# Last spline of a graph network: records loaded once the points have used them, GpSimd waiting for the spreads itself, and late picks standing in front of the wait for a spread

## What is computed

```
new_pseudo = jnp.clip(pseudo + t[col] - t[row], 0.0, 1.0)
basis2, idx2 = spline_basis(new_pseudo)        # 3 coordinates, 5 hats each: 125 weights, 8 of them not zero
z = jnp.einsum('ni,kio->nko', x, W)            # W: [125, 32, 32]
msg = jnp.einsum('es,eso->eo', basis, z[col * 125 + idx])
out = segment_sum(msg, row) / max(degree, 1) + b
```

## Time and profile before

| what | us |
|---|---|
| median of 3 runs (range) | 6453.58 (6439.67 to 6467.0) |
| the profiled execution, its own time | 6460.42 |
| its span, first to last instruction | 6458.6 |
| first gather of this stage starts | 5155.21 |
| first gather after it that waited for a load (block 7) | 5371.20 |
| last gather of this stage starts, takes | 6347.66, 0.94 |
| first `pos` of block 0, of block 1 | 5215.94, 5238.55 |
| first `pos` of block 36, the last | 6379.35 |

### The profile page before, as it was taken

How to read it: one execution, slowest core, us unless ns; L and a number is a source line. 1 busy time by engine, 2 the same in 40 slices (tenths; PEclk the granted TensorE clock), 3 DMA queues, 4 the chain that set the end, 5 groups by cost and what they waited for, 6 DMA issues and landing times. The chain is left out here.

```text
span 6458.6 us, 112027 instructions
## 1 busy us (share of the span) xinstructions
PE 4758.0 (74%) x38171; PEld 3579.6 (55%) x38171; DVE 4337.5 (67%) x11010; ACT 1867.2 (29%) x3181; POOL 4196.4 (65%) x4245
## 2 busy tenths in 40 slices
PE   5444444493668988888885755999999678888885
PEld 4444444363656766666664343555555366666664
DVE  7665565366888877777773222777777477788875
ACT  0212111254884444444442000000000033333332
POOL 1777777406946777777772533777777377777773
PEclk9999999987999999989887877999999889999998
DMA  4222222014442222222223946111111211111110
GB/s 69 87 74 79 81 74 71 18 34 118 169 164 49 58 59 57 58 55 57 58 55 101 325 142 189 38 38 37 37 37 37 37 19 22 22 22 22 22 22 16
DMA packets 387137, 441.07 MB, mean 68 GB/s; under 512 B 244355, under 2 KB 310736, under 8 KB 386397
## 3 DMA queue, kind: packets, MB, share of 16 engines
q1 hardware_dynamic: 202041, 290.11, 14.3%
q0 software_dynamic: 128224, 124.94, 11.5%
q10 hardware_dynamic: 56528, 21.19, 1.6%
HBM read 354.14 MB, written 82.34 MB: 68 GB/s over the span
## 5 line engine op out<-in xcount | busy, mean ns | idle before, releaser
L886 POOL DMA_INDIRECT ar_far<-att_table,ar_rec x1184 | 1210.4, 1022 | 422.8 <-issue 352.6
L1726 POOL DMA_INDIRECT p_far<-table,p_rec x888 | 866.2, 975 | 417.3 <-issue 262.2
L2564 PE MATMUL g_l_ps_sum<-g_l_row,g_l_of 128*128 128x392 f32 x3224 | 1064.5, 493 | 19.4 <-DVE g_l_of L2515 19.4
L2486 POOL DMA_INDIRECT g_l_got<-table,g_l_index x806 | 812.6, 1008 | 245.5 <-issue 227.8
L550 POOL DMA_INDIRECT rec_r<-so_r_rec,so_r_place x806 | 788.1, 978 | 245.5 <-issue 245.2
L2564 PEld LDWEIGHTS g_l_ps_sum<-g_l_row,g_l_of 128*128 128x128 f32 x3224 | 613.9, 190 | 470.5 <-DVE g_l_of L2515 20.5
L1500 PE MATMUL at_bank<-p_spread,p_basis 64*125 64x256 f32 x4736 | 624.1, 410 | 99.1 <-ACT p_outer L1562 99.1
L505 PE MATMUL so_r_look<-so_r_table,so_r_lo_t 128*128 128x26 f32 x1612 | 424.9, 434 | 313.2 <-DVE so_r_table L447 313.2
L2498 DVE TENSOR_SCALAR g_l_row<-g_l_iota,edge_row 128x784 f32<-128x784 f32 x806 | 500.4, 694 | 230.9 <-PE g_l_ps_sum L2564 230.8
L1500 PEld LDWEIGHTS at_bank<-p_spread,p_basis 64*125 64x125 f32 x4736 | 525.4, 196 | 179.3 <-ACT p_outer L1562 122.8
L1562 ACT COPY p_outer<-at_bank 125x512 f32<-125x512 f32 x1184 | 592.2, 715 | 101.2 <-PE at_bank L1500 100.6
(11 more groups left out here) (493 smaller groups left out, 6946.6 us busy)
## 6 DMA issues: line engine op xcount, KB each, us to landing
adjacent<-ad_by_chunk SPq DMA_DIRECT2D x74, 800.0 KB, 3.3
so_r_row<-pad_src SPq DMA_DIRECT2D x62, 832.0 KB, 6.1
g_l_counts<-adjacent SPq DMA_DIRECT2D x60, 800.0 KB, 7.1
g_l1d_counts<-adjacent SPq DMA_DIRECT2D x59, 800.0 KB, 6.8
so_r_low<-pad_lo_src SPq DMA_DIRECT2D x62, 416.0 KB, 4.6
ar_far<-att_table,ar_rec POOLq DMA_INDIRECT x1184
p_far<-table,p_rec POOLq DMA_INDIRECT x888
rec_r<-so_r_rec,so_r_place POOLq DMA_INDIRECT x806
```

The lines of the kernel that those rows point to most:

```text
L886: pool.indirect_dma_start(out=self.far[q][:, t, :], out_offset=None, in_=self.g.att_table[:, :], in_offset=bass.IndirectOffsetOnAxis(ap=se ...
L1726: pool.indirect_dma_start(out=sl.far[b][:, t, :], out_offset=None, in_=table[:, :], in_offset=bass.IndirectOffsetOnAxis(ap=sl.rec[b][:, t, ...
L2486: pool.indirect_dma_start(out=got[b][:, j, :], out_offset=None, in_=table[:, :], in_offset=bass.IndirectOffsetOnAxis(ap=index[b][:, j:j + ...
L2564: last = nc.tensor.matmul(ps_sum[k][:], of4[b][:, j, :, :].rearrange("p k f -> p (k f)"), row1[b][:, j, k * COLS:(k + 1) * COLS], start=Fa ...
```

## The change

Three edits in this stage, none of them in arithmetic:

1. In `outer_products`, the late picks (tiles 8 and 20) are issued before TensorE waits for the spread of these tiles, where they stood behind that wait.
2. SP loads block `n`'s records as soon as `positions` says that the points of block `n - 3` have read them, where it waited for that block's last spread.
3. GpSimd, from block 3 on, waits itself for the spreads of block `n - 3` (the readers of `far[b]`) after it has waited for the records. Its first three blocks are therefore written out ahead of its loop, and the loop starts at lap 1.

```diff
             if t % self.HT == 0:
                 pe.wait_ge(self.bases, m * 2 + (t // self.HT + 1))
+            if late is not None and t in (8, 20):
+
+                late[0].pick(pe, m + 1, 2 + (t == 20))
             if t % self.XT == 0:
                 pe.wait_ge(self.spreads, m * self.XS + (t // self.XT + 2))
...
             if turn_of is not None and t == self.HT - self.BT:
                 self.turn(pe, turn_of)
-            if late is not None and t in (8, 20):
-
-                late[0].pick(pe, m + 1, 2 + (t == 20))
...
                 with sp.Fori(1, turns) as i:
                     for b in ring:
-                        sp.wait_ge(sl.spreads, i * (R * sl.XS) + ((b - R + 1) * sl.XS + 1))
+                        sp.wait_ge(sl.positions, i * R + (b - R + 2))
                         sl.load(sp, i * R + b, b)
                 for n in range(turns * R, o.blocks):
-                    sp.wait_ge(sl.spreads, (n - R + 1) * sl.XS + 1)
+                    sp.wait_ge(sl.positions, n - R + 2)
                     sl.load(sp, n, n % R)
...
-                def gather(i, b):
+                def gather(i, b, first=False):
                     pool.wait_ge(sl.loaded[b], i * sl.loads + sl.loads)
+                    if not first:
+                        pool.wait_ge(sl.spreads, i * (R * sl.XS) + ((b - R + 1) * sl.XS + 1))
                     pool.sem_inc(taken, 1)
...
-                with pool.Fori(0, turns) as i:
+                for b in ring:
+                    gather(0, b, first=True)
+                with pool.Fori(1, turns) as i:
                     for b in ring:
                         gather(i, b)
```

## The result

| | before | changed |
|---|---|---|
| median (range) | 6456.01 us (6439.67 to 6467.0), 4 runs | 6397.74 us (6390.22 to 6399.57), 4 runs |
| ratio of the medians, 95% interval | | 0.9904 (0.9886 to 0.9923) |
| the profiled execution, its span | 6460.42, 6458.6 | 6390.22, 6388.2 |
| first gather of the stage | 5155.21 | 5144.57 |
| `pos` of block 1, of block 36 | 5238.55, 6379.35 | 5226.52, 6309.27 |

The kernel became faster by about 58 us where 74 were forecast, and the time lies inside the range. The spans differ by 70.4 us, but 10.6 of them lie ahead of the stage, which no edit touches: in the profiled executions of this study its first gather starts anywhere from 5132.02 to 5168.05. From here on I compare the 35 blocks between the `pos` of block 1 and that of block 36 ("the 35 blocks"): they lost 58.05 us, and the tail behind them kept its 79 us.

What follows compares the result with a forecast made beforehand. DVE and PE, waiting on each other through the late picks, were taken as the bound, GpSimd hidden. Waits 59 plus clock 15 gave 74 us off the profiled 6460.4, so 6386, median 6379; range 6360 to 6410.

Steps and rivals of the forecast that it cites:

- waits for spreads before picks: PE's waits for DVE's spreads ahead of late picks, 81.8 us over the stage, would go, less what stays or comes new.
- the new wait for spread 3: On PE ahead of tiles 12 to 15: 0.4 us a block in 22 blocks, as DVE makes one-hots before that spread.
- Edit 1: Late picks on PE start sooner: block 15 falls from 33.04 to 29.4 us, the stage gains 59 + 15 = 74.
- The clock: PE's picks return from half to full clock after shorter idleness: 15 us of gain, bounds 22 and −15.
- The 22 us in picks 2: Time lost to half clock in the picks 2 of 15 blocks that followed a long wait on PE.
- The factor of 0.7: Share taken of the clock's 22 us, giving 15, since block 16 shows PE meeting half clock elsewhere too.
- Rival 1: PE falls to half clock at the loop's start or another pick as often: gain 42 to 62 us, chance 0.22.
- Edits 2 and 3: Loads and GpSimd's wait: up to 64.9 us of POOL's idleness go, but by themselves they are worth nothing.
- Rival 2: GpSimd's wait costs more than SP's and bounds: 6396 us at 0.8 a block; chance 0.08 part, 0.03 slower.
- The cap: GpSimd's gather work ends no sooner than 6291.9, so block 36's points start 6298 to 6301: gain at most 78 to 85 us.
- Rival 3: Something other than the pick, such as ScalarE, holds tiles 20 to 23: gain 20 to 40 us, chance 0.09.
- Rival 4: Order of picks does nothing because kept products come as late as the spreads: time 6454, chance 0.03.

Runs made afterwards that it cites:

- edit 1 alone: Kernel before with only the late picks issued ahead of the wait for their spread, loads and GpSimd's wait as before: 6392.03 us, ratio 0.9893.
- the laps of six: Changed kernel with TensorE's loop written out for six blocks a lap instead of three: 6395.53 us, ratio 0.9896 against the kernel before.
- the shifts ahead: Changed kernel with the near shifts and the turn also issued ahead of the wait for spread 3 at tile 12: 6384.76 us, ratio 0.9879.
- the one-hots later: Kernel with near shifts and turn ahead of tile 12's wait, VectorE making one-hots behind spread 3 instead of ahead: 6382.25 us, ratio 0.9871.
- pick 3 late again: Changed kernel with tile 20's pick back behind the wait for its spread, tile 8's still ahead: 6416.23 us, ratio 0.9924.
- filling the gap before pick 2: Kernel before, products of tile 7 issued eight times over in all but a lap's first block: 6455.80 us, ratio 0.9981.

## Why the prediction was right, and where 16 us went

The sum can be checked term by term against groups by line, of the kernel before from 5238 to 6380 us (two that the earlier trace rows doesn't hold):

```profile
L1500 PE MATMUL p_ps_outer<-p_spread,p_basis 64*125 64x128 f32 x4510 | 316.1, 284 | 35.5 <-issue 25.3 <-DVE p_spread L1434 7.3
...
L1528 PE MATMUL p_ps_rest<-p_fold,p_run 128*128 128x32 f32 x140 | 22.1, 281 | 0.0
```

and of the changed kernel from 5226 to 6310 us:

```profile
L1680 PE MATMUL p_pick_ps_pick<-p_pick_parts,p_pick_turned_hot 128*128 128x245 bf16 x3360 | 398.7, 276 | 71.6 <-DVE p_pick_kept L1653 71.6
L1500 PE MATMUL p_ps_outer<-p_spread,p_basis 64*125 64x128 f32 x4510 | 313.4, 283 | 31.0 <-issue 22.8 <-DVE p_spread L1434 6.0
L1528 PE MATMUL p_ps_rest<-p_fold,p_run 128*128 128x32 f32 x140 | 23.4, 292 | 0.0
L1464 PE MATMUL p_ps_rest<-p_shift,mask_t 8*128 8x96 f32 x70 | 15.9, 306 | 30.3 <-DVE p_spread L1434 30.2
```

| term | forecast | measured |
|---|---|---|
| waits for spreads before picks, gone | 81.8 | 81.8 |
| more waiting for kept products (71.6 − 57.2) | −22 × 0.65 = −14.3 | −14.4 |
| the new wait for spread 3 | −22 × 0.4 = −8.8 | −30.2 |
| idleness ahead of products (35.5 − 31.0) | 0 | 4.5 |
| clock: picks 13.4, products 2.7, turn −1.3 | 15 | 14.8 |
| sum | 74 | 56.5 |

Of the 58.05 us that the blocks lost, 1.5 aren't attributed by this.

**Edit 1: the mechanism was right.** Pick 2 waits at most 0.71 us for a kept product, spread 4 doesn't stall, and the gain comes from PE starting late picks sooner. **The step that failed in size** is "Here a new wait stands: spread 3 ends at 5718.44, ... so PE waits 0.4 us". I let the near shifts and the turn run beside this wait, though in the code they stand behind it, and they take 0.94 us. So where nothing else delays PE the wait is 1.3 to 1.4 us instead of 0.4, and it comes in 30 blocks and not in the 22 that I counted: 30.2 us against 8.8, which is the missing 16 us and more. Putting the two calls ahead brought the wait down to 0.38 and gave 20.2 us back in the 35 blocks: shown. That kernel, at 78.2 us saved, is even above the 74. DVE's stall before spread 7 was 2.99 us instead of 2 for the same 0.94.

**The clock: right in size by luck, and differently made up.** 15 taken, 14.8 measured. But kernels with the picks in the same places spread around that: by the same reckoning edit 1 alone has 11.5 us and the laps of six 18.0. The 22 us in picks 2 came back whole, and the start of a lap ran at full clock (2.02) too. What took part of it back are picks 1 at half clock (3.9 to 4.4 us in blocks 9, 12, 15, 18, 21, 24, 27 and 30; in three blocks before), and tiles 12 to 19 in blocks 1, 5, 8 and 11. The factor of 0.7 stood for such places without naming them.

**Rival 1** (the clock doesn't come back) gave 42 to 62 us and 6391 to 6411. The measured 58 us and 6397.74 lie in its band, and not in the forecast's own 62 to 90 us and 6364 to 6392: the time is inside the stated range because that had been widened for this rival. Its mechanism is seen in part, in the picks 1, but it isn't what kept the gain down, since the clock gave the 15 us that were forecast; the wait for spread 3 did.

**Edits 2 and 3: right**, worth nothing alone, nor on top of edit 1 (1082.75 against 1085.11 us), nor with the shifts ahead. **Rival 2** was wrong: GpSimd's wait costs nothing that its rows show, 0.3 us between gathers at block borders as elsewhere. The working had 1136.7 us for its gathers without any wait, and from 5144.57 the last one ended at 6281.43, 1136.9 later. The cap (block 36's points not before GpSimd's work is done) was right, and decides once the blocks save 80 us. **Rival 3** was wrong, as tiles 20 to 23 were held by the pick: in block 15 spread 7 comes 3.87 us behind the start of pick 3, and 3.86 before. **Rival 4** was wrong too, since pick 2 did start sooner.

**The median** fell by 58 us and not by the 70.4 of the spans, as the profiled execution of the changed kernel had 10.6 us less ahead of the stage. The forecast had put the one of before 6.8 above its median.

## What to carry to other kernels

When a wait is freed of what stands needlessly behind it, read the program for every further wait on that path and list what is issued behind each, since the next one then decides: here the neighbour held 0.94 us of work that needed nothing of it, and moving that too was worth 16 to 20 us after 58. Count the new wait in all blocks, not in those where the old one was long. A saving of idle time on TensorE was here a saving of clock too, but the half clock then turned up behind other gaps, so a clock's part should be taken from the kernel's total and not from one block.

The best kernel here is the changed one with the shifts ahead (6384.76 us; with the one-hots later 6382.25, not distinguishable). Both beat the kernel before clearly, and the change by 16 to 20 us, which single executions and ratios support but whose intervals touch. Beyond them GpSimd's gathers have to become fewer or shorter.

## What the runs showed of the hardware

- The same code meets the half clock in a rhythm of its own: behind the same wait of 1.44 us the changed kernel ran tiles 12 to 19 in 3.78 us in block 5 and in 2.02 in block 17. Between kernels that differ in one place it stands in other blocks (four in the changed kernel, 13 with pick 3 late again, nine starts of a lap with the shifts ahead, slow picks 1 not counted). Why a given gap does it isn't settled; the runs settle only that filling the gap before pick 2 removed it there.
- The jump back of TensorE's loop shows as 2.0 to 3.4 us of idleness ahead of the first matmul behind it, and is gone in blocks where laps of six have taken the jump away.
- Gathers that follow each other without a pause, 0.94 us and 0.30 between, kept on beside VectorE's work: their mean was 976 ns after and 975 before.
- The first gather of the stage starts up to 36 us apart between kernels that don't differ ahead of it (5132.02 to 5168.05), which is why a stage's own length, and not the span, was compared.
